# ScalarE's order around the softmax weights, and one context load moved up, in a one-core perceiver kernel

## The reference, cut to what matters

```
q = split_heads(x @ Wq) * 64 ** -0.5
k, v = split_heads(context @ Wkv)            # plus one null key and one null value
attn = softmax(q @ k.T)                      # 8 batches x 16 heads, 64 x 1602
out = (attn @ v) @ Wout, then a layer norm
```

## Time and profile before

| | |
|---|---|
| three runs | 3096.91, 3099.53, 3100.01 us; median 3099.53 us |
| profiled execution | 3094.91 us, its span 3093.2 us, mean TensorE clock 0.957 |
| busy in the span | TensorE 2789.4 us (90%), DVE 1966.0 (64%), ACT 1186.8 (38%), GpSimd 820.1 (27%) |
| `attend` | from 1329 us of the span; its last scores' attention ends near 2615 us |

### The profile page before, as it was taken

How to read it: one execution, slowest core, us unless ns; L and a number is a source line. 1 busy time by engine, 2 the same in 40 slices (tenths; PEclk the granted TensorE clock), 3 DMA queues, 4 the chain that set the end, 5 groups by cost and what they waited for, 6 DMA issues and landing times. The chain is left out here.

```text
span 3093.2 us, 52547 instructions
## 1 busy us (share of the span) xinstructions
PE 2789.4 (90%) x21561; PEld 1835.2 (59%) x21569; DVE 1966.0 (64%) x2478; ACT 1186.8 (38%) x1853; POOL 820.1 (27%) x594
## 2 busy tenths in 40 slices
PE   6999999998989999979999999999999973796799
PEld 3334444443434444469989888989898962334453
DVE  5358999994554788845666666666666653368410
ACT  3254343331433444423444444444444432174210
POOL 1000000000000655545555555555555510100000
PEclk9999999999999999989999999999999996887899
DMA  5033343334332444321555555555555556101203
GB/s 202 26 123 93 88 129 116 91 96 153 123 99 92 150 130 126 113 85 45 126 146 131 131 133 138 133 135 133 136 131 131 131 135 152 59 0 28 109 16 134
DMA packets 471365, 343.88 MB, mean 111 GB/s; under 512 B 231923, under 2 KB 441140, under 8 KB 466646
## 3 DMA queue, kind: packets, MB, share of 16 engines
q1 hardware_dynamic: 471126, 340.52, 39.2%
HBM read 230.27 MB, written 55.67 MB: 92 GB/s over the span
## 5 line engine op out<-in xcount | busy, mean ns | idle before, releaser
L1895 PE MATMUL ca_p_k<-early_region,early_r 128*128 128x201 f16 (+1 forms) x2048 | 516.4, 252 | 18.8 <-DVE early_region L1871 8.2
L1896 PE MATMUL ca_p_k<-early_region,early_r 128*128 128x201 f16 (+1 forms) x2048 | 512.6, 250 | 0.0
L1897 PE MATMUL ca_p_k<-early_region,early_r 128*128 128x201 f16 (+1 forms) x2048 | 512.4, 250 | 0.0
L1895 PE MATMUL ca_p_k<-early_region 128*128 128x201 f16 (+1 forms) x1536 | 385.8, 251 | 38.6 <-DVE ca_held L1920 38.6
L1897 PE MATMUL ca_p_k<-early_region 128*128 128x201 f16 (+1 forms) x1536 | 382.9, 249 | 0.0
L1896 PE MATMUL ca_p_k<-early_region 128*128 128x201 f16 (+1 forms) x1536 | 382.8, 249 | 0.0
L1920 DVE TENSOR_TENSOR ca_held<-ca_p_k,ca_held 128x402 f32<-128x402 f32 (+1 forms) x448 | 245.0, 567 | 122.6 <-PE ca_p_k L1897 122.4
L390 PE MATMUL vw_pv<-vw_wv,vw_ctx 128*128 128x512 f16 (+1 forms) x688 | 263.9, 384 | 35.1 <-PEq L74 15.3
L391 PE MATMUL vw_pv<-vw_wv,vw_ctx 128*128 128x512 f16 (+1 forms) x688 | 263.7, 383 | 0.0
L392 PE MATMUL vw_pv<-vw_wv,vw_ctx 128*128 128x512 f16 (+1 forms) x688 | 263.6, 383 | 0.0
L1938 ACT ACTIVATE ca_store<-ca_held 128x804 f16<-128x804 f32 (+2 forms) x128 | 112.0, 875 | 326.7 <-DVE ca_held L1920 322.0
(11 more groups left out here) (571 smaller groups left out, 6324.1 us busy)
## 6 DMA issues: line engine op xcount, KB each, us to landing
vd<-vw_vst SPq DMA_DIRECT2D x192, 256.0 KB, 2.3
ca_vals<-vd SPq DMA_DIRECT2D x64, 768.0 KB
vw_ring<-in_ctx_t SPq DMA_DIRECT2D x89, 512.0 KB, 3.9
x<-in_ctx_k SPq DMA_DIRECT2D x32, 804.0 KB, 4.9
early_region<-in_ctx_k SPq DMA_DIRECT2D x32, 804.0 KB, 6.5
ex_w_d<-in_w_d SPq DMA_DIRECT2D x8, 2048.0 KB, 7.9
vw_ring<-in_w_kv SPq DMA_DIRECT2D x16, 512.0 KB, 4.4
early_r<-state_rows SPq DMA_DIRECT2D x8, 1024.0 KB, 7.1
```

What stands on the lines that cost most here:

```text
L1895: self.nc.tensor.matmul(o[:, e, :], w[:, 0, c, f], x[:, 0, k], start=(c == 0), stop=False)
L1896: self.nc.tensor.matmul(o[:, e, :], w[:, 0, c, f], x[:, 1, k], start=False, stop=False)
L1897: last = self.nc.tensor.matmul(o[:, e, :], w[:, 1, c, f], x[:, 0, k], start=False, stop=(c == self.HALF - 1))
```

## The change

In a step that serves a pair, ACT writes `weights_high` directly behind the exponentials and then the split of product 1 (even) or product 5 (odd); before, that split stood between the two. The second context half of the first quad gets its own place in `region` (behind three of the eight slots, which are laid around it), over a weight table (`t[0]`) that V's product 2 reads. SP loads it inside V's last quad, after three products of that quad are done and ahead of the quad's outputs. The load at the top of `attend` is gone.

```
+RAW_AT = 3 * CC * KN
...
-    def sp(self, sp):
+    def sp(self, sp, behind_t1):
...
+            if i == vw.QUADS - 1:
+                sp.wait_ge(self.s_prod, 7 * i + 3)
+                behind_t1()
             for k, (t, g) in enumerate(self.OUTS):
                 sp.wait_ge(self.out_lo, 4 * i + k + 1)
...
-            sp.dma_start(first_raw, io.ctx_k[0, 0, 0, :, :]).then_inc(ld_first, 16)
+            sp.dma_start(first_raws[0], io.ctx_k[0, 0, 0, :, :]).then_inc(ld_first[0], 16)
             vw.sp(sp, LAST_UNITS)
-            quads.sp(sp)
+            quads.sp(sp, lambda: sp.dma_start(first_raws[1], io.ctx_k[0, 0, 1, :, :]).then_inc(ld_first[1], 16))
...
-        self.raws = [first_raw.rearrange("p (h n) -> p h n", h=2), carve.take([P, 2, self.WIDE])]
-        self.slots = [carve.take([P, 2, self.WIDE], f16) for s in range(self.SLOTS)]
+        self.raws = [x.rearrange("p (h n) -> p h n", h=2) for x in first_raws]
+        self.slots = [carve.take([P, 2, self.WIDE], f16) for s in range(3)]
+        carve.at = RAW_AT + 2 * CC * KN
+        self.slots += [carve.take([P, 2, self.WIDE], f16) for s in range(3, self.SLOTS)]
...
         for t in range(2):
-            if i or t:
+            if i:
                 sp.dma_start(self.raws[t]...
...
-            kw.load(sp, 0)
             sp.dma_start(nk, io.null_k).then_inc(ld_null, 16)
...
                 if f >= 0:
                     exps(f)
-                if t < PARTS:
-                    kw.high(act, i + 1, 5 if later else 1)
-                if f >= 0:
                     weights_high(f)
                 if t < PARTS and not later:
+                    kw.high(act, i + 1, 1)
                     kw.high(act, i + 1, 2)
                 elif t < PARTS:
+                    kw.high(act, i + 1, 5)
                     kw.out_high(act, i, 2)
                     kw.high(act, i + 1, 6)
                     kw.out_high(act, i, 3)
```

More of the change, by code:

```diff
@@ L1647, with queries @@
 P_UP = 4096.0
-def queries(nc, io, k, vw, x, xn, xt, q_parts, region, tk, first_raw, x_saved, ld_first):
+def queries(nc, io, k, vw, x, xn, xt, q_parts, region, tk, first_raws, x_saved, ld_first):
     with Stage(nc, "cq") as st:
@@ L1761, with __init__ @@
     OVER_OUT = {0: 4, 1: 3, 3: 2}
-    def __init__(self, nc, io, st, tk, rest, first_raw, ld_first, scored, banks):
+    def __init__(self, nc, io, st, tk, rest, first_raws, ld_first, scored, banks):
         self.nc, self.io, self.tk, self.banks, self.scored = nc, io, tk, banks, scored
         carve = Carve(rest)
-        self.raws = [first_raw.rearrange("p (h n) -> p h n", h=2), carve.take([P, 2, self.WIDE])]
-        self.slots = [carve.take([P, 2, self.WIDE], f16) for s in range(self.SLOTS)]
+        self.raws = [x.rearrange("p (h n) -> p h n", h=2) for x in first_raws]
+        self.slots = [carve.take([P, 2, self.WIDE], f16) for s in range(3)]
+        carve.at = RAW_AT + 2 * CC * KN
+        self.slots += [carve.take([P, 2, self.WIDE], f16) for s in range(3, self.SLOTS)]
         self.spare = carve.take([P, 2, P], f16)
@@ L1774, in __init__ @@
             self.null_in = st.sems("s_made op_hi op_lo s_lo prod copied added out_hi out_lo null_in")
-        self.ld = [ld_first, st.sem("ld_raw1")]
+        self.ld = ld_first
     def cell(self, b, p, q):
@@ L1949, in null_key, with attend @@
                 self.nc.vector.tensor_copy(o, nk[:, None, None, :].to_broadcast([P, 2, 2, 2])).then_inc(self.null_in, 1)
-def attend(nc, io, k, x, q_parts, o_t, vd, tk, rest, first_raw, ld_first, quads):
+def attend(nc, io, k, x, q_parts, o_t, vd, tk, rest, first_raws, ld_first, quads):
     with Stage(nc, "ca") as st:
@@ L1955, in attend @@
         scored = st.sem("scored")
-        kw = KeyWork(nc, io, st, tk, rest, first_raw, ld_first, scored, [p_k[:, i * BANK:(i + 1) * BANK] for i in range(KeyWork.BANKS)])
+        kw = KeyWork(nc, io, st, tk, rest, first_raws, ld_first, scored, [p_k[:, i * BANK:(i + 1) * BANK] for i in range(KeyWork.BANKS)])
         probs = st.sb("probs", [P, KEYS])
@@ L3417, in build @@
                   .rearrange("p (l c n) -> p l c n", l=2, c=CC // 2) for r in range(7)]
-            x_saved, ld_first = early.sems("x_saved ld_first")
-            first_raw = x[:, :, :].rearrange("p t d -> p (t d)")[:, 0:CC * KN]
+            x_saved = early.sem("x_saved")
+            ld_first = [early.sem(f"ld_raw{t}") for t in range(2)]
+            first_raws = [x[:, :, :].rearrange("p t d -> p (t d)")[:, 0:CC * KN],
+                          region[:, 24 * 512 + RAW_AT:24 * 512 + RAW_AT + 2 * CC * KN].bitcast(f32)]
             with Stage(nc, "vw") as st:
@@ L3424, in build @@
                 bitnet(nc, io, k, vw, x, xn, xt, r1, region)
-                queries(nc, io, k, vw, x, xn, xt, q_parts, region, tk, first_raw, x_saved, ld_first)
-            attend(nc, io, k, x, q_parts, o_t, io.vd, tk, region[:, 24 * 512:], first_raw, ld_first, vw.quads)
+                queries(nc, io, k, vw, x, xn, xt, q_parts, region, tk, first_raws, x_saved, ld_first)
+            attend(nc, io, k, x, q_parts, o_t, io.vd, tk, region[:, 24 * 512:], first_raws, ld_first, vw.quads)
         project_out(nc, io, k, x, o_t)
```

## The result

The changed kernel took a median of 3070.48 us (five runs, 3066.25 to 3076.21) against 3099.53: a ratio of 0.991 [0.9896, 0.9923], 29 us less where 19.4 were forecast, and inside the predicted range. Lines moved: 1863 is now 1869, 1871 is 1877, 1854 is 1860, 1895 is 1901, 1920 is 1926, 1942 is 1948, 2133 is 2138, 2179 is 2183, 2186 is 2190.

The account below looks back on a forecast made before the run. TensorE was taken as nearly always busy from 1330 to 2490 us, so only its gaps could be won. -41.4 + 27.8 - 4.1 - 1.7 = -19.4 us gave 3080.1 from 3099.5; own range 3072 to 3089, overall 3051 to 3092.

Parts of the forecast that it names:

- Even steps: Paired even steps: earlier weights remove all 26 TensorE waits for a DVE add at product 4, -41.4 us.
- the 2.24 won: Even step: `weights_high` starts 2.24 us earlier, at the inverse plus 0.12, and `weights_low` comes 2.24 earlier too.
- Odd steps: Odd steps: GpSimd's low part of product 5 delays `out_low`(2); TensorE newly waits 1.03 us in 27 steps, +27.8 us.
- The cover: Odd step: slack between add(6,0) and half 1 of the next quad, beyond the handover; 0.30 us against 1.33 of delay.
- First load: Start of `attend`: GpSimd begins with the stage and its third sum ends 4.1 us earlier, -4.1 us.
- Clock: After the longest wait: the one fall of the granted clock, 0.97 over 58 us, would not occur, -1.7 us.
- The tail: After the last quad: its own order is unchanged and it shifts whole.
- (1): Odd step: DVE goes first or GpSimd's low part comes too late to block; no 27.8 loss, 3052.3 us, chance 0.22.
- (2): Little left: GpSimd's two copies also precede `out_low`(2), or transposes hold `weights_high`; 3097 us, chance 0.12.
- the third: Slower: GpSimd's low part of product 1 precedes `weights_low`, odd steps' late load comes through; 3116.4 us, chance 0.08.

Follow-up runs that it names:

- even order alone: Kernel before, with only the even steps' split of product 1 moved behind `weights_high`; odd steps and load as before: 3050.08 us, ratio 0.9857.
- GpSimd's work gone: Changed kernel, but from quad 5 on GpSimd makes only 8 of 804 columns of product 5's low part: 3047.87 us, ratio 0.9854 to the kernel before.
- load alone: Changed kernel with ACT's old order, so only the early load of the second context half is new: 3091.44 us, ratio 0.9997 to the kernel before.
- odd order alone: Kernel before, with only the odd steps' split of product 5 moved behind `weights_high`: 3105.21 us, ratio 1.0041.
- the repeat: Changed kernel run a second time without edit: 3072.08 us, ratio 0.993 to the kernel before.
- add first: Changed kernel with add(6,0) ahead of `out_low`(2) on DVE in odd steps: 3043.06 us, ratio 0.9837 to the kernel before.
- no odd half: Changed kernel with product 5's split ahead of `weights_high` again; even order and early load kept: 3051.11 us, second time 3048.64 us.

## Why the prediction was right

- **Even steps, -41.4.** Measured 42.8 in the 52 steps, the clock's term inside it (41.4 + 1.7 = 43.1 by the prediction). What the prediction overlooked is GpSimd's third sum in the way of `weights_low` (2.39 to 3.12 us in 10 of 27 steps); the 2.24 won had room for it. Shown by the even order alone. To count a wait from one before and after, 0.17 more than its stated length, was needed to come this near: the stated waits alone sum to 37.0.
- **Odd steps, +27.8.** The mechanism is shown from three sides: taken alone, with the add ahead, and with GpSimd's work gone. The term was mis-sized: 23.1 in 26 steps, 0.89 a step in place of 1.03; with the tail's odd step 24.0 for 27. The difference has a place. `out_low`(2) ends 2.42 after `weights_low`, just the row that the prediction took. But it counted that end 1.33 us later than before; after the inverse it ends at 6.16 in place of 4.89 in the mean of the steps, 1.27 later, and add(6,0) 1.26 later, for `weights_low` is over 0.16 earlier and not 0.10, its row now 1.89 long and not 1.96. The cover was then 0.37 in place of the 0.30 read at one step.
- **First load, -4.1.** Measured 4.6 (145.03 to 140.46). The third sum came 4.38 earlier. The last V quad did not pay: from its first late output on DVE (1319.59 before, 1320.92 after) to ACT's first split in `attend` it is 9.62 us in both.
- **Clock, -1.7.** The fall at 2088 is gone, and it was not peculiar to one execution. Each of the three kernels that have the even waits shows one fall in its paired steps, behind its longest wait (2.5, 2.4 and 2.2 us: before, load alone, odd order alone), with 0.97 over 58 us in each. The seven profiles without them have none there, the odd waits of up to 1.2 us included. Waits do not all end so: one of 2.26 us in the kernel before is followed by no fall.
- **The tail, 0.** From the last of the 52 steps to the stage's end it is 146.1 before and 147.3 after: 0.9 is the 27th odd step, which the prediction had counted in its 27. The other 0.3 is not explained; this end took 145.3 to 147.5 in the ten profiles.
- **The sum.** -42.8 + 23.1 - 4.6 + 1.2 = -23.1 us in `attend`, against -19.4: 3.7 more, about what the odd term was too large by (27.8 to 24.0, 3.8). The rest of the first measurement's 29 lies in stages that were not changed, the head attention above all, and did not come again: 21.5 in the repeat. So the first median, 1.5 us below the forecast's own range of 3072 to 3089, owes that to them and not to a term of the sum.
- **The rivals.** That DVE goes first (1) fell with `out_low` at 2.50 in the profile after. The copies of GpSimd (2) did not go ahead: 2.50 is below the 3.1 that it needed. Of the third, the late load was there, 0.8 us. GpSimd's low part of product 1 did not get in before `weights_low`: it starts 0.8 after the other's start, as worked out, or later. GpSimd's third sum did, in 10 steps. The 2.24 won on the weights absorbed both: even-to-odd steps are at TensorE's own 18.01.

The Trainium skill ("SBUF — State Buffer", section "Who interferes with whom") has DVE and GpSimd contend as described above and exempts a DVE instruction with at most one input in SBUF, outside modes that use both port pairs; the add has its other input in PSUM, and its 0.57 us beside GpSimd's 2.62 agrees.

What stays open: why the granted clock of the head attention differs between executions of unchanged code, and so whether 3043.06 (add first) and 3048.64 (no odd half) differ by more than that: their paired steps take the same 936.9 and 936.7 us.

## What to carry to other kernels

An order that helps in one step of a loop need not help in its sibling: read the waiting instruction in each before both are changed. Where GpSimd's operation can come due during a long DVE instruction on SBUF, put the DVE work that TensorE waits for, if it reads PSUM, next in DVE's queue, and work with no haste behind it. When a gain of 1% is measured, compare the stage that was changed first: here some 6 of 29 us came from stages in which not a line differs.

## What the runs showed of the hardware

- A GpSimd operation that comes due during a DVE instruction on SBUF goes ahead of DVE's next one on SBUF, in all 27 odd steps: `out_low`(2) lasts 2.50 with 804 columns pending on GpSimd, 2.02 with an add of 0.57 in between, 0.99 with 8 columns. With 804 columns it ends 0.85 us after GpSimd's operation in either order.
- It holds up DVE the other way as well: where GpSimd's third sum is at work when `weights_low` comes, this one's row is 2.39 to 3.12 us long in place of 1.89, in 10 of the 27 even steps of the changed kernel.
- The recorded start of a GpSimd row is not when it got its turn: 8 columns have a row of 1.11 us that begins during `weights_low` and ends 0.06 behind it.
- The wait shows in DVE's row too, at the stage's start: its split begins at 1331.52 in GpSimd's first sum, which ends at 1332.49, and ends at 1333.34, 0.85 after it.
